# Keeping the running sums of layer 0 in one SBUF tile from the second attention to the last stage

## The reference

```python
x = L0_attn_x                                     # (32, 256, 128)
xn = _layernorm(x)
x = x + _L0_attn_ref(xn, ...) + _L0_ffn_ref(xn, ...)   # top-1 of 8 experts, hidden 512
xn = _layernorm(x)
x = x + _L1_attn_ref(xn, ...) + _L1_ffn_ref(xn, ...)   # shared expert + softmax-gated top-2 of 8
return x
...
def _L1_ffn_ref(...):
    shared = jnp.einsum('td,dh->th', x_flat, shared_w1.T)
    shared = jnp.einsum('th,hd->td', jax.nn.silu(shared), shared_w2.T)
    ...
    selected = jnp.einsum('ted,te->td', expert_out, gates)
    return (shared + selected).reshape(B, S, D)
```

## Time and profile before

| | us |
|---|---|
| time, median of 3 runs | 1695.55 |
| lowest and highest of them | 1689.3, 1696.78 |
| the profiled execution: its time | 1693.03 |
| its span | 1691.3 |
| PE, DVE, POOL, ACT busy in the span | 1392.7, 1242.4, 1029.3, 885.9 |

### The profile page before, as it was taken

One profiled execution on the slowest core, in us unless ns is written; L12 is line 12 of the kernel. 1 busy time (PEld: TensorE's weight loads), 2 busy tenths in 40 slices (PEclk: granted clock), 3 DMA queues, 4 the chain that ended last, 5 costly groups with the idle time before them and its releaser, 6 DMA issues. The chain is left out here.

```text
span 1691.3 us, 42035 instructions
## 1 busy us (share of the span) xinstructions
PE 1392.7 (82%) x14758; PEld 1078.4 (64%) x14759; DVE 1242.4 (73%) x2603; ACT 885.9 (52%) x1437; POOL 1029.3 (61%) x746
## 2 busy tenths in 40 slices
PE   7858999999999999998189968888888099999940
PEld 5635666666666666665179966667667099999940
DVE  5559999999999999998356646999998523333346
ACT  7818888888888888887034422222222044444420
POOL 6624888888888888889534432656556544444420
PEclk9859999999999999999589988999999599999975
DMA  6863333333333333310533321222221122222248
GB/s 221 270 197 95 77 83 82 83 82 84 82 82 83 84 80 86 81 50 18 138 123 99 94 60 59 90 94 82 89 93 54 50 63 68 66 65 65 65 138 289
DMA packets 117937, 163.58 MB, mean 97 GB/s; under 512 B 18592, under 2 KB 85408, under 8 KB 113184
## 3 DMA queue, kind: packets, MB, share of 16 engines
q1 hardware_dynamic: 92960, 123.42, 26.3%
q0 software_dynamic: 13600, 28.45, 5.1%
q10 hardware_dynamic: 11232, 9.73, 1.8%
HBM read 99.52 MB, written 62.01 MB: 96 GB/s over the span
## 5 line engine op out<-in xcount | busy, mean ns | idle before, releaser
L921 ACT ACTIVATE Ex<-pB 128x512 f32<-128x512 f32 x512 | 514.3, 1081 | 84.5 <-PE pB L731 80.2
L962 POOL TENSOR_TENSOR V<-Ex,R 128x4096 f32<-128x4096 f32 x64 | 474.2, 7409 | 98.8 <-DVE R L841 98.7
L819 DVE TENSOR_REDUCE mg<-pA 128x128 f32<-128x1024 f32 x256 | 297.5, 1203 | 3.7 <-PE pA L714 3.4
L835 DVE TENSOR_REDUCE Z<-Ex 128x64 f32<-128x2048 f32 x128 | 290.7, 2273 | 4.6 <-ACT Ex L921 4.5
L731 PEld LDWEIGHTS pB<-qk 72*128 72x128 bf16 x2048 | 157.7, 97 | 122.5 <-issue 1.1
L726 PE MATMUL pB<-mh,identb 128*128 128x512 bf16 x512 | 196.6, 384 | 36.0 <-ACT Ex L921 35.4
L1113 POOL DMA_INDIRECT y_d<-x1yb,x1xb x136 | 130.2, 957 | 151.4 <-DVE x1yb L1228 146.8
L731 PE MATMUL pB<-qk 72*128 72x128 bf16 x2048 | 198.9, 219 | 0.0
L726 PE MATMUL pB<-ml,identb 128*128 128x512 bf16 x512 | 194.0, 379 | 0.0
L741 PE MATMUL pO<-V,Vh 128*8 128x128 f32 x4096 | 161.0, 278 | 12.9 <-POOL V L962 12.8
L714 PE MATMUL pA<-qk 72*128 72x128 bf16 x2048 | 162.5, 224 | 8.8 <-DVE mg L819 4.9
(11 more groups left out here) (232 smaller groups left out, 2368.1 us busy)
## 6 DMA issues: line engine op xcount, KB each, us to landing
qk<-qs_d SPq DMA_DIRECT2D x96, 192.0 KB
qk<-ks_d SPq DMA_DIRECT2D x96, 192.0 KB
x1xb<-xs_d SPq DMA_DIRECT2D x136, 64.5 KB
f_ye<-y_d SPq DMA_DIRECT2D x16, 512.0 KB, 5.9
qs_d<-parts SPq DMA_DIRECT2D x16, 384.0 KB, 2.9
ks_d<-parts SPq DMA_DIRECT2D x16, 384.0 KB, 3.2
x0xb<-xs_d SPq DMA_DIRECT2D x72, 64.5 KB
xn_d<-xn SPq DMA_DIRECT2D x16, 258.0 KB, 3.3
```

The lines of the kernel that those rows point to most:

```text
L819: dve.tensor_reduce(mg[:, :, g], pA[:, g % 2, :, :].rearrange("p b q -> p q b"), AX.X, ALU.max).then_inc(b_red, 1)
L835: dve.tensor_reduce(Z[:, q], Ex[:, j, q, :], AX.X, ALU.add).then_inc(b_sum, 1)
L921: act.activation(Ex[:, j, :, BG * g:BG * (g + 1)].rearrange("p q b -> p b q"), pB[:, g % 2, :, :], ACT.Exp).then_inc(b_exp, 1)
L962: pool.tensor_tensor(En[:, j % 2, :, :].rearrange("p b q -> p q b"), Ex[:, j, :, :], R[:, j % 2, :].unsqueeze(2).broadcast_to([P, P, B]), ...
```

## The change

A tile `x2` of 128 x 64 x 128 in SBUF (32 KB in each partition) is allocated ahead of stage `d` and lives until the end. `rows_of(t)` is the part of it that belongs to tile t. Stage `d` loads x into it and works on it where `d_acc` stood; the stores to `x2_d` are gone, and with them SP's waits for the last addition and for the stores to land. Stage `f` adds to the same tile and stores from it; the loads of the sums are gone. SP now holds back the load of `f_ye` for tile t until DVE has finished tile t-4 (`f_2`), and no longer until its output store has landed. `d_acc` and `f_acc`, 8 KB in each partition in their stages, are gone.

```diff
--- before.py
+++ after.py
@@ -125,7 +125,6 @@
     V_d = nc.dram_tensor("V_d", [H, P, NS, DK], F32).ap()
     V_p = V_d.rearrange("h p n d -> p h n d")
     oT_p = oT_d.rearrange("d (u r) -> d u r", u=2)
-    x2_d = nc.dram_tensor("x2_d", [P, NS, D], F32).ap()
 
 
     xs0_d = nc.dram_tensor("xs0_d", [E * REG + SPARE * P, DR], F32).ap()
@@ -1250,12 +1249,17 @@
 
 
 
+        x2 = sb("x2", [P, NS, D])
+
+        def rows_of(t):
+
+            return x2[:, t * SUB:(t + 1) * SUB, :]
+
         with ExitStack() as ph:
             rt = routing_tiles("d", ph, TOPK)
             idx = sb("d_idx", [P, 4, TOPK, SUB], U32, ph)
             oT = sb("d_oT", [P, 2, TT], F32, ph)
             ye = sb("d_ye", [P, 2, SUB, D], F32, ph)
-            acc = sb("d_acc", [P, 4, SUB, D], F32, ph)
             xn = sb("d_xn", [P, 4, TOPK, SUB, DR], F32, ph)
             xnT = sb("d_xnT", [P, 2, TT], F32, ph)
             st = sb("d_st", [P, SUB, 6], F32, ph)
@@ -1314,7 +1318,6 @@
             d_ln = sem("d_ln")
             d_ys = sem("d_ys")
             d_acc = sem("d_accs")
-            d_x2 = [sem(f"d_x2{i}") for i in range(4)]
             WS = 2 * E
             LINKS = 3
             LINKS1 = 2 * 5 + 3 + 2 * SUB + 1 + 3 * TOPK
@@ -1323,15 +1326,7 @@
 
             @block.sync
             def _(sp):
-                def store(t, q):
-                    sp.wait_ge(d_acc, t + 1)
-                    settle(sp, settled)
-                    sp.dma_start(x2_d[:, bass.ds(t * SUB, SUB), :], acc[:, q, :, :]).then_inc(d_x2[q], 16)
-
                 def body(t, q):
-                    if started(t, 4):
-                        sp.wait_ge(d_x2[q], 4 * (t - q))
-                        settle(sp, settled)
                     if started(t, 2):
                         sp.wait_ge(d_wo, t - 1)
                         settle(sp, settled)
@@ -1341,15 +1336,9 @@
                                  oT_p[:, :, bass.ds(t * 2 * P, 2 * P)]).then_inc(d_x[q], 16)
                     sp.dma_start(ye[:, q % 2, :, :].rearrange("p (u b) d -> p u b d", u=2),
                                  y0_v[:, :, bass.ds(t * 2, 2), :]).then_inc(d_x[q], 16)
-                    sp.dma_start(acc[:, q, :, :].rearrange("p (u b) d -> p u b d", u=2),
+                    sp.dma_start(rows_of(t).rearrange("p (u b) d -> p u b d", u=2),
                                  x_p[:, :, bass.ds(t * 2, 2), :]).then_inc(d_x[q], 16)
-                    if started(t, 3):
-                        store(t - 3, (q + 1) % 4)
                 sweep(NT, body, 4)
-                for t in range(NT - 3, NT):
-                    store(t, t % 4)
-                for q in range(4):
-                    sp.wait_ge(d_x2[q], 4 * NT)
 
             @block.tensor
             def _(pe):
@@ -1485,12 +1474,12 @@
 
                     s = q % 2
                     dve.wait_ge(d_x[q], 12 * (t - q) + 48)
-                    dve.tensor_tensor(acc[:, q, :, :], acc[:, q, :, :], ye[:, s, :, :], ALU.add).then_inc(d_sum, 1)
+                    dve.tensor_tensor(rows_of(t), rows_of(t), ye[:, s, :, :], ALU.add).then_inc(d_sum, 1)
                     dve.wait_ge(d_wo, t + 1)
                     dve.wait_ge(d_sum, t + 1)
-                    dve.tensor_tensor(acc[:, q, :, :], pC[:], acc[:, q, :, :], ALU.add).then_inc(d_x1, 1)
+                    dve.tensor_tensor(rows_of(t), pC[:], rows_of(t), ALU.add).then_inc(d_x1, 1)
                     dve.wait_ge(d_x1, t + 1)
-                    row_statistics(dve, st[:], mv[:], acc[:, q, :, :], d_st, t, settled).then_inc(d_agg, 1)
+                    row_statistics(dve, st[:], mv[:], rows_of(t), d_st, t, settled).then_inc(d_agg, 1)
 
                 def norm(t, q):
                     dve.wait_ge(d_rs, t + 1)
@@ -1500,7 +1489,7 @@
                         dve.tensor_copy(xn[:, q, i, :, D:DR].bitcast(U32),
                                         dest1[:, i, bass.ds(t * SUB, SUB)].unsqueeze(2))
                     for j in range(SUB):
-                        ins = dve.tensor_scalar(xn[:, q, 0, j, 0:D], acc[:, q, j, :], mv[:, j, 0:1], rs[:, j:j + 1],
+                        ins = dve.tensor_scalar(xn[:, q, 0, j, 0:D], rows_of(t)[:, j, :], mv[:, j, 0:1], rs[:, j:j + 1],
                                                 ALU.subtract, ALU.mult)
                     ins.then_inc(d_xn, 1)
 
@@ -1535,7 +1524,7 @@
                     link(dve.tensor_tensor(o[:], o[:], lnw[:].unsqueeze(1).broadcast_to([P, SUB, D]), ALU.mult))
                     link(dve.tensor_tensor(o[:], o[:], lnb[:].unsqueeze(1).broadcast_to([P, SUB, D]), ALU.add))
                     dve.wait_ge(d_ys, t + 1)
-                    dve.tensor_tensor(acc[:, q, :, :], acc[:, q, :, :], o[:], ALU.add).then_inc(d_acc, 1)
+                    dve.tensor_tensor(rows_of(t), rows_of(t), o[:], ALU.add).then_inc(d_acc, 1)
 
                 def body(t, q):
                     s = q % 2
@@ -1561,7 +1550,7 @@
                     if started(t, 1):
                         finish(t - 1, (q + 3) % 4)
                     dve.wait_ge(d_y, t + 1)
-                    dve.tensor_tensor(acc[:, q, :, :], pY[:], acc[:, q, :, :], ALU.add).then_inc(d_ys, 1)
+                    dve.tensor_tensor(rows_of(t), pY[:], rows_of(t), ALU.add).then_inc(d_ys, 1)
                     dve.wait_ge(d_o, t + 1)
                     if started(t, 1):
                         dve.wait_ge(d_acc, t)
@@ -1628,7 +1617,6 @@
             low = sb("f_low", [P, NS], F32, ph)
             gt = sb("f_gt", [P, 4, TOPK, SUB], F32, ph)
             ye = sb("f_ye", [P, 4, SUB, TOPK, D], F32, ph)
-            acc = sb("f_acc", [P, 4, SUB, D], F32, ph)
             f_x = [sem(f"f_x{i}") for i in range(4)]
             f_i = sem("f_i")
             f_gate = sem("f_gate_s")
@@ -1643,9 +1631,8 @@
             def _(sp):
                 def body(t, s):
                     if started(t, 4):
-                        sp.wait_ge(f_out[s], 4 * (t - s))
+                        sp.wait_ge(f_2, t - 3)
                     settle(sp, settled)
-                    sp.dma_start(acc[:, s, :, :], x2_d[:, bass.ds(t * SUB, SUB), :]).then_inc(f_x[s], 16)
                     sp.dma_start(ye[:, s, :, :, :], y1_v[:, bass.ds(t * SUB, SUB), :, :]).then_inc(f_x[s], 16)
                 sweep(NT, body, 4)
 
@@ -1660,11 +1647,11 @@
 
                 def body(t, s):
                     dve.wait_ge(f_i, t + 1)
-                    dve.wait_ge(f_x[s], 8 * (t - s) + 32)
+                    dve.wait_ge(f_x[s], 4 * (t - s) + 16)
                     for i, done in enumerate((f_1, f_2)):
                         for j in range(SUB):
-                            ins = dve.scalar_tensor_tensor(acc[:, s, j, :], ye[:, s, j, i, :],
-                                                           gt[:, s, i, j:j + 1], acc[:, s, j, :],
+                            ins = dve.scalar_tensor_tensor(rows_of(t)[:, j, :], ye[:, s, j, i, :],
+                                                           gt[:, s, i, j:j + 1], rows_of(t)[:, j, :],
                                                            ALU.mult, ALU.add)
                         ins.then_inc(done, 1)
                         if i == 0:
@@ -1686,7 +1673,7 @@
             def _(act):
                 def body(t, s):
                     act.wait_ge(f_2, t + 1)
-                    act.dma_start(out[:, bass.ds(t * SUB, SUB), :], acc[:, s, :, :]).then_inc(f_out[s], 16)
+                    act.dma_start(out[:, bass.ds(t * SUB, SUB), :], rows_of(t)).then_inc(f_out[s], 16)
                 act.wait_ge(f_gate, 1)
                 act.activation(low[:], low[:], ACT.Exp).then_inc(f_exp, 1)
                 sweep(NT, body, 4)
```

## The result

| | kernel before | with the change |
|---|---|---|
| median of 5 runs, us | 1689.6 | 1676.36 |
| lowest, highest | 1688.11, 1696.78 | 1674.47, 1678.89 |
| span of the profiled execution | 1691.3 | 1672.4 |
| first SP issue of the last stage to the end of the span | 58.1 | 43.9 |

The ratio of the new time to the old is 0.9919 (95% interval 0.9898 to 0.9941): 13.7 us less by the ratio, 13.2 by the two medians. Two more runs of the kernel before had moved its median from 1695.55 to 1689.6, and the forecast had been taken from the first.

What follows compares the result with a forecast made beforehand. The last stage was taken as a four-buffer ring held by waits and nearly by bytes, with DVE the next bound. Its end, 1677.4 + 1.1 = 1678.5 against 1691.3, saves 12.8 us: 1695.55 - 12.8 = 1682.7 us, range 1677 to 1689.

Steps and rivals of the forecast that it cites:

- Stage `d`: Stage `d`: removing the stores and their waits brings 0 us, since loads were already early and the last store is covered.
- DVE's additions in their new place: Same addition instructions on a larger SBUF tile: 0 us, as L1491 took 690 to 692 ns over four buffers.
- DVE becomes the bound: Last stage: with the landing wait gone, DVE's 2.37 us a tile sets the pace, 37.9 us for 16 tiles.
- Can the bytes keep up?: Last stage: DVE wants 332 GB/s and 337 are to be had; 1.1 us taken for waits left.
- a second road: Last stage's end by subtracting DVE's waits from the old span: 1677.8 beside 1676.9; the middle, 1677.4, was used.
- rival with slow bytes: Last stage: load and store mix runs at 275 GB/s, so bytes bound it; 6.6 us less, 1689 us; chance 0.08.
- bunched loads: Last stage: loads queue and land after 8.1 us, the ring still waits; 9.9 us less, 1685.7 us; chance 0.12.
- slow large tile: Both stages: new addresses slow DVE's operations by 19%; whole kernel 9.6 us slower, 1705 us; chance 0.02.
- no effect: Last stage: the ring's wait only hides another, so the edit does nothing; 1695 us; chance 0.02.
- The rules of the Trainium skill: Last stage: 358 GB/s gives 13.9 to 14.4 us saving; DMA anatomy prices the removed wait at 7.8 us, trace 15.2.
- How the numbers follow: Whole kernel: forecast chance 0.76, faster 0.88, within half a per cent 0.09, slower 0.03; range 1677 to 1689 us.

## Why the prediction was right, and where it was not

- *Stage `d`*: 0 us, right. The loads of its fifth tile are 14 us earlier against the stage's start, as foreseen, and nobody was waiting for them; with the stores put back the ratio stays the same (0.9912).
- *DVE's additions in their new place*: 0, right (692 ns in both).
- *DVE becomes the bound*: right. Its 16 tiles took 37.7 us (forecast 37.9), the tail 2.5 (2.5), the start from SP's first issue 3.7 (3.3). That makes 43.9 us against a floor of 43.7.
- *Can the bytes keep up?* This term was mis-sized. I had taken 313 / 0.93 = 337 GB/s as what the engines give when never idle, so two limits seemed to lie together, and I left 1.1 us for waits and moved the floor up by 0.5 us by a second road. That made 45.3 us for the stage (58.1 - 12.8), 1.4 us more than the 43.9 measured. Measured: 398 and 410 GB/s at a share of 1.03, and no wait behind the first tile. A DMA share near 1 did not mean that the engines were at their limit: with the change it is 0.97 at 326 GB/s, about what DVE asks for (332). A byte took 15% more of the engines' recorded time there than at 398 GB/s (0.97 / 326 against 1.03 / 398). The rival with slow bytes (275 GB/s) leant on the same mistake, and so had too much of a chance. The prediction also calls 337 the mean of the windows; over the 40 us it was 313, and 337 is that divided by the share.
- *The bunched loads, the slow large tile and no effect*: none came. The landings had a median of 4.8 us and at most 6.2, not 8.1; the additions kept their 692 and 347 ns; and the stage lost 14.2 us.
- *The rules of the Trainium skill*: its 358 GB/s for a core ("DMA: Bandwidth & Descriptors", specifications) is, by the same page's bandwidth section, the share with both cores of a pair streaming. It is below what two kernels moved on this one core for 24 and 30 us on end; the 436 GB/s on which its anatomy of one DMA builds is nearer. The saving that the prediction worked out under the 358, 13.9 to 14.4 us, fits the 14.2 us of the stage better than the forecast does, since under it DVE had room to spare. The anatomy is of DMAs that GpSimd issues; the stores here are issued by ScalarE, and the shortest landed in 2.0 us, less than the 2.6 that it gives for their 256 KB. The price that the prediction took from it for the removed wait, 7.8 us, is also what removing the wait last measured, 14.2 - 6.4 = 7.8 us. That is luck: the chain with the wait kept has a store of 5.98 us, not of 2.6.
- *How the numbers follow*: this is the step of the prediction that failed. The saving was held against 1695.55, the median of three runs, two of which were high; 4 us were left for scatter, though the lowest of the three lay 6 us under that median. Against the 1689.6 of five runs the same 12.8 us would have given 1676.8, 0.4 us from the result. So of the 6.3 us between the forecast (1682.7) and the result, 5.95 are the level, and the 1.4 us of the term above hardly show in the medians. The later 14 and 10 runs of the kernel before, beside other kernels, had medians of 1689.09 and 1690.46, near the 1689.6. Two places of scatter were found: the first stage (up to 7 us in the `xr` load) and the granted clock in the last tile of stage `d` (3.3 us).

## What to carry to other kernels

Where a buffer is loaded, worked on and stored in a ring, ask which of the three the next load really has to wait for: data that are kept elsewhere take the store out of the ring, and the ring's round, divided by the buffers, tells when that stops to matter. Don't read a transfer limit off a stretch in which something else sets the pace; make a kernel in which nothing does. And a forecast for a kernel whose runs scatter by half a per cent should be a difference first, with a range for the level that spans the runs shown.

## What the runs showed of the hardware

- The 16 DMA engines moved 410 GB/s (two loads and a store a tile) and 398 GB/s (one load and one store) over 30 and 24 us, and showed a share of 1.03 there; at 326 GB/s, with DVE setting the pace, they showed 0.97. The share can't tell the two apart.
- A load of 512 KB took 3.8 to 4.6 us to land, median 4.3, even with only two buffers, where at 398 GB/s its bytes need 1.3 us.
- The granted clock of TensorE fell to 0.50 in the last tile of stage `d` in some executions and not in others, at the same program and after the same 2.93 us without work; four matmuls then took 3.75 us and not 1.96.
